# The second pass's mask of four heads copied into the bank by ScalarE, a third bank for its scores, and a third slice ahead of the projection

## The reference, cut to what matters

```python
scores = jnp.einsum('bhcqd,bhckd->bhcqk', qc, kb) / jnp.sqrt(jnp.asarray(d, q.dtype))
...
allowed = mb[:, None, :, None, :] & pos_ok[None, None, :, None, :] & band_ok[None, None, None, :, :]
scores = jnp.where(allowed, scores, jnp.asarray(-1000000000.0, scores.dtype))
probs = jax.nn.softmax(scores, axis=-1)
out = jnp.einsum('bhcqk,bhckd->bhcqd', probs, vb)
```

## Time and profile before

| | |
|---|---|
| median of 3 runs | 5509.81 us (5508.85 to 5511.06) |
| profiled execution, its own time | 5544.22 us |
| its span, first to last instruction | 5542.4 us |
| granted TensorE clock, mean | 0.978 of full speed |
| TensorE busy | 5064.9 us (91%) |
| VectorE busy | 3498.0 us (63%) |
| ScalarE busy | 2573.6 us (46%) |
| GpSimd busy | 1152.9 us (21%) |

### The profile page before, as it was taken

How to read it: one execution, slowest core, us unless ns; L and a number is a source line. 1 busy time by engine, 2 the same in 40 slices (tenths; PEclk the granted TensorE clock), 3 DMA queues, 4 the chain that set the end, 5 groups by cost and what they waited for, 6 DMA issues and landing times. The chain is left out here.

```text
span 5542.4 us, 119208 instructions
## 1 busy us (share of the span) xinstructions
PE 5064.9 (91%) x41842; PEld 3972.4 (72%) x41842; DVE 3498.0 (63%) x8963; ACT 2573.6 (46%) x5128; POOL 1152.9 (21%) x1048
## 2 busy tenths in 40 slices
PE   0799999999999999999999999969999954999999
PEld 0577777777777777777777777747777742777766
DVE  6566666666666666666666666567777745333332
ACT  0355555555555555555555555535555630111111
POOL 6111111111111111111111111100000001545453
PEclk9999999999999999999999999989999976999999
DMA  6544444444444444444544444344444420333232
GB/s 106 105 88 92 97 92 89 107 93 98 91 88 90 103 101 95 89 88 94 105 101 88 90 97 94 67 93 96 92 101 95 95 69 17 65 83 81 67 87 41
DMA packets 1283995, 488.94 MB, mean 88 GB/s; under 512 B 1086659, under 2 KB 1270560, under 8 KB 1283872
## 3 DMA queue, kind: packets, MB, share of 16 engines
q1 hardware_dynamic: 1256224, 450.63, 37.3%
q0 software_dynamic: 27648, 36.72, 4.3%
HBM read 162.82 MB, written 60.28 MB: 40 GB/s over the span
## 5 line engine op out<-in xcount | busy, mean ns | idle before, releaser
L764 ACT ACTIVATE pT<-banks 128x384 f32<-128x384 f32 x1920 | 924.9, 491 | 768.8 <-PE banks L533 758.1
L982 DVE TENSOR_REDUCE mx<-banks 128x4 f32<-128x768 f32 x768 | 719.4, 950 | 294.3 <-PE banks L514 294.3
L1165 POOL TENSOR_TENSOR rstd<-ve,half 128x2 f32<-128x2 f32 x288 | 218.8, 760 | 3062.4 <-DVE ve L891 3062.4
L496 PE MATMUL banks<-maskb,eyeb 128*128 128x384 bf16 (+1 forms) x2304 | 719.0, 312 | 91.6 <-DVE mx L986 27.0
L514 PE MATMUL banks<-qkT 128*128 128x192 bf16 (+2 forms) x3840 | 633.5, 247 | 0.0
L533 PE MATMUL banks<-qkT 128*128 128x192 bf16 (+2 forms) x3840 | 630.8, 247 | 0.0
L632 PE MATMUL banks<-w,pT 128*128 128x192 f32 x3072 | 554.5, 330 | 0.0
L632 PEld LDWEIGHTS banks<-w,pT 128*128 128x128 f32 x3072 | 492.7, 190 | 42.4 <-issue 21.9
L496 PE MATMUL banks<-mseq,eyeb 128*128 128x384 bf16 x1536 | 501.9, 327 | 9.1 <-issue 4.4
L618 PE MATMUL banks<-nT,w 128*128 128x256 f32 x1920 | 472.5, 382 | 6.6 <-DMA b<-in_b 3.1
L1910 PE MATMUL ps_g<-exp_xT,exp_wg 64*128 64x512 f32 x1152 | 466.8, 600 | 10.8 <-issue 5.4
(11 more groups left out here) (202 smaller groups left out, 8745.1 us busy)
## 6 DMA issues: line engine op xcount, KB each, us to landing
hcur<-hbuf SPq DMA_DIRECT2D x164, 192.0 KB
resid<-hbuf SPq DMA_DIRECT2D x160, 192.0 KB, 2.5
amb<-am_d SPq DMA_DIRECT2D x130, 192.0 KB, 3.0
hbuf<-hout SPq DMA_DIRECT2D x128, 192.0 KB, 2.0
exp_wg<-in_ewg SPq DMA_DIRECT2D x16, 768.0 KB
exp_wu<-in_ewu SPq DMA_DIRECT2D x16, 768.0 KB
exp_wd<-in_ewd SPq DMA_DIRECT2D x16, 576.0 KB
xs<-xr SPq DMA_DIRECT2D x32, 272.0 KB, 2.2
```

Of the source, the lines that this page charges most:

```text
L496: nc.tensor.matmul(part(dst), eyeb[:], part(mask), start=True, stop=ph is not tok)
L764: ph.inc(nc.scalar.activation(pT[s][:, h % NPT, :], bank[s][h % 2][:, 0:SCOLS], ACT.Exp, scale=SCALE), "p", s)
L982: last = nc.vector.tensor_reduce(mx[s][:, :, at].rearrange("p t h -> p h t"), src[:, :, 0:SCOLS].rearrange("p h (t k) -> p h t k", t=T), A ...
```

## The change

Four heads of K's second pass (7, 8, 9 and 11) get their mask from ScalarE, in the token layers only. After the Exp of head 6, ScalarE copies `mseq` into the banks of heads 7, 8 and 9, and after the Exp of head 10 into that of head 11; a new semaphore `wm` tells TensorE, which adds the two score matmuls to what stands there. The second pass of the token layers goes through banks 0, 1 and 3 in turn, so a head that TensorE masks waits for the Exp of head h-3. And of the six slices of the feed-forward three instead of two stand in front of the projection, here and in the causal block.

```diff
-UP_BEGIN = (0, 1)
-UP_REST = (2, 3, 4, 5)
+UP_BEGIN = (0, 1, 2)
+UP_REST = (3, 4, 5)
...
+WRITTEN = {6: (7, 8, 9), 10: (11,)}
+WRITTEN_HEADS = (7, 8, 9, 11)
...
+        def keys_bank(ph, s, h):
+            return bank[s][(0, 1, 3)[h % 3] if ph is tok else h % 2]
+
         def pe_scores2(ph, pe, K, V, h, kcols):
             s = K.s
+            written = ph is tok and h in WRITTEN_HEADS
+            ahead = 3 if ph is tok else 2
...
-            if h >= 2:
-                ph.wait(pe, "p", s, K.it, h - 1)
-            dst = bank[s][h % 2]
-            pe_mask(ph, dst, mseq[s] if ph is tok else maskb[:, 3, :])
+            dst = keys_bank(ph, s, h)
+            if written:
+                ph.wait(pe, "wm", s, K.it, WRITTEN_HEADS.index(h) + 1)
+            elif h >= ahead:
+                ph.wait(pe, "p", s, K.it, h + 1 - ahead)
+            if not written:
+                pe_mask(ph, dst, mseq[s] if ph is tok else maskb[:, 3, :])
...
-                ph.inc(nc.scalar.activation(pT[s][:, h % NPT, :], bank[s][h % 2][:, 0:SCOLS], ACT.Exp, scale=SCALE), "p", s)
+                ph.inc(nc.scalar.activation(pT[s][:, h % NPT, :], keys_bank(ph, s, h)[:, 0:SCOLS], ACT.Exp, scale=SCALE), "p", s)
+                for later in WRITTEN.get(h, ()) if ph is tok else ():
+                    ph.wait(act, "p", s, K.it, later - 2)
+                    ph.inc(nc.scalar.copy(keys_bank(ph, s, later)[:, 0:SCOLS], mseq[s][:]), "wm", s)
```

More of the change, by code:

```diff
@@ L441, in tower @@
         tok = Phase(layer_sems, dict(
-            common, tb=2, am_in=16, ms=1, ml=MASK_LINKS, hb2=1, w1_ps=FC, g=FC, w2_ps=1, r2=1, var2=1, rstd2=1, h2=1,
+            common, tb=2, am_in=16, ms=1, wm=len(WRITTEN_HEADS), ml=MASK_LINKS, hb2=1, w1_ps=FC, g=FC, w2_ps=1, r2=1, var2=1, rstd2=1, h2=1,
             h_st=16, sl=TOK_STACK_LINKS, fl=MAX_LINKS, bl=TOK_BACK_LINKS, b2=FFN_LINKS), "t",
@@ L534, in pe_scores2 @@
                                         qT[s][:, h, f0:f0 + w], start=False,
-                                        stop=(t == T - 1), skip_group_check=ph is not tok)
+                                        stop=(t == T - 1), skip_group_check=ph is not tok or written)
             ph.inc(last, "sc2", s)
```

## The result

The changed kernel takes 5434.83 us (5433.18 to 5438.39, 4 runs), the kernel before on the same chip 5510.44 (5508.85 to 5511.4): a ratio of 0.9864, 95% interval 0.9847 to 0.9881. That is 75.6 us less, where I forecast 69, and 5435 against 5441.

The account below looks back on a forecast made before the run. TensorE's issue was taken to bound the token stage; masks 0.36 plus slice 0.21 made 0.57 us a half, times 119 halves 68, plus 1 causal: 69 us off 5509.8, so 5441 us, likeliest range 5430 to 5456.

Parts of the forecast that it names:

- The factor of 119 halves: Of 128 token halves, 119 keep the gain; the last two and some 7 around layer changes do not.
- The masks: Token halves: four masks free 0.65 us of TensorE; waits of 0.07 (head 8) and 0.21 (head 10) leave 0.36.
- The copies: ScalarE's four mask copies per token half: 0.49 us each, spaced 0.39, costing nothing on the path.
- The price that the prediction put on slower copies: Slower rival, long copies into banks: gain gone at 0.7 us a copy, 1.2 us a half lost at 1.0; chance 0.04.
- The slice: Third slice before the projection removes TensorE's stall there for hT: 0.21 us a half, 0 if it only moves.
- The cover of the delayed norm: Behind the projection, residual and norm end 0.22 us later; 1.2 us remain before TensorE transposes h1.
- The sum: 0.36 + 0.21 = 0.57 us a half; over 119 halves 68 us, plus 1 in the causal stage: 69 us.
- ScalarE was not the limit: Rival: copy and Exp don't overlap, each taking 0.49 us; gain 0.34 a half, 40 us, 5469; chance 0.12.
- the slice gave its part: Rival: the third slice before the projection gives nothing; 0.36 a half, 43 us, 5467; chance 0.07.
- DMA didn't move in: Rival: DMA sets the pace, mT landing late and holding each half at some 0.2 of gain; 5486; chance 0.04.
- VectorE would be no limit: Rival: VectorE's maxima move too, so 0.86 us a half is gained, 102 us, 5408; chance 0.03.
- The granted clock: Waits of 0.07 and 0.21 shouldn't lower TensorE's clock; rival: half clock for parts of each half, 5630; chance 0.02.

Follow-up runs that it names:

- pool_late: The changed kernel, with POOL making the next masks only after all six row maxima of that half: 5404.50 us, 0.9805 of the kernel before.
- copy_twice: The changed kernel, with ScalarE copying each mask first into a spare tile nobody reads: 5554.35 us, 1.0081 of the kernel before.
- slice_only: The kernel before with only the third slice in front of the projection, masks and banks unchanged: 0.9942 of the kernel before (5509.99 us against 5543.66 us).
- three_masks: The changed kernel with head 11's mask given back to TensorE (ScalarE writes 7, 8, 9): 0.9868 of the kernel before (5470.92 us against 5543.66 us).
- five_masks: The changed kernel with head 6's mask also written by ScalarE, after the Exp of head 3: 5423.17 us, 0.9842 of the kernel before.

## Why the prediction was right, step by step

**What bounds.** TensorE's issue in the token stage, up to the dates that VectorE's maxima set: borne out by the runs; each change of a half's length in the traces is in the times. The factor of 119 halves was an estimate. By the traces the token stage gained some 123 times what a half gained here, and 122 times in `pool_late`.

**The masks**, 0.36 a half forecast. Head 10 came 0.362 and 0.363 earlier, with the two waits at their forecast places and sizes (0.07 and 0.21). Behind it half of the halves lose more: the transposes of hcur came 0.351 earlier in the first kind and 0.308 in the second, so 0.011 and 0.055 is lost there. I had them meet the fifth maximum to 0.01 us and took 0.01. `pool_late`, in which the fifth maximum comes earlier too, has both losses gone. In the mean the masks gave 0.330, 0.03 less than forecast.

**The copies**, 0.49 with a spacing of 0.39 forecast: 0.484 in the mean and 0.41 in the changed kernel, and no wait for them. `copy_twice` shows the cover and its end, and the walk made for it held within 3 us. The price that the prediction put on slower copies is too high: the gain gone at 0.7 us a copy and 1.2 lost at 1.0, so by the same slope of four 0.8 lost at 0.9, or 95 us. With 0.41 more for every copy, so about 0.9 each, a half was 0.435 and 0.362 longer than before, and the kernel 43 us slower. A straight line between the two kernels puts the break-even at about 0.73 (my estimate; no run measured it).

The Trainium skill ("ScalarE: Activation LUTs", What ACT_TABLE_LOAD costs) gives 186 ns plus 0.833 ns an element for an ACTIVATE with immediate operands, and an overlap of about 93 ns between two in a row. An estimate from these is 506 ns for 384 elements and a spacing of 0.41. The trace has 484 ns for the copy, which is what counts here, and the same spacing.

**The banks**: nothing forecast, 0.9993 of before measured.

**The slice**: 0.21 forecast. It is 0.206 in the first kind of half and 0.28 in the second (0.280 by the changed kernel's halves, 0.277 by `slice_only`), where the projection used to wait 0.08 longer. I had read one half of the first kind only. So this term was mis-sized too: 0.243 in the mean, 4 us in all. The cover of the delayed norm held: no wait of TensorE for h1 is in the waits.

**The sum.** 0.557 and 0.588 a half, 0.572 in the mean, against 0.57: the slice's surplus of 0.033 and the masks' shortfall of 0.030 cancel, so that the half came out this close is luck; the two mechanisms are not. The token stage gave 70.2 us by the two traces, where 68 was forecast, the causal stage 1.7 against 1, and the passage between them lost 1.4. That is 70.5 of the 75.6 us measured; the rest is inside the interval (66 to 84 us) and I can't assign it. The causal 1.7 isn't firm either: that stage takes 812.9 to 813.1 us in the three profiles with two slices ahead of the projection, and 810.2 to 813.2 in the eleven with three, 813.1 in `slice_only` among them.

**The profiled execution** was expected at 5473 and came out at 5431.4 because I took the profile's 34 us above the median for its own; they belong to the chip it was taken on.

**The rivals.** ScalarE was not the limit (0.41, not 0.49 a copy), the slice gave its part, DMA didn't move in. That VectorE would be no limit was out by `three_masks`. The granted clock stayed at 1.00 in both stretches above. Inside the four layers it was half for 3.4 us twice in the profile of the kernel before and twice in that of the changed one, each time just behind an idle of TensorE of 2.0 to 2.6 us around a change of layer, and not behind the waits of 0.07 and 0.21. The Trainium skill's rule on cycling through banks ("TensorE: Matmul & The Clock Gate", A second HAM failure mode: psum-queue depth-cycling) isn't seen at work in the halves of these two profiles.

**What I had not seen.** I wrote that behind the third maximum VectorE works without a break, and read its rows as its own time. This line of the profile before stands beside the centring (2015.02 to 2016.50) in the earlier trace rows:

```profile
2015.16 1.12 POOL L1175 TENSOR_TENSOR mseq<-maskf,amb 128x384 bf16<-128x384 f32 x1
```

Half of the centring's 1.48 us goes when POOL's mask is moved away. The forecast's dates came out, since the third maximum and the centring behind it don't move with the change. But the limit that took 0.21 us from each half was one of POOL against VectorE, and it could be had back for one wait: 31 us.

## What to carry to other kernels

A matmul taken out of a full TensorE is worth its slot only up to the next date that another engine sets; walk the half forward and look for these dates, because in front of such a wait a removed mask was worth 0 us, and 22 once the wait was gone. A spare half of an engine's span says nothing about a stretch: four copies were free and four more cost 118 us. Read both kinds of a repeating unit before sizing a stall.

## What the runs showed of the hardware

Two f32 instructions of 128 x 192 on VectorE (scalar_tensor_tensor, both tensors in SBUF) take 0.41 us each alone. In the changed kernel POOL's tensor_tensor of 128 x 384 runs beside both. The first meets it for its last 0.27 us and still takes 0.41; the second starts 0.18 behind POOL's start, takes 1.16 and ends 0.21 behind POOL's end, and POOL's takes 1.12 instead of 1.00. With POOL elsewhere the second is back to 0.41 in every half. The Trainium skill ("GPSIMD Engine Reference", the SBUF interfaces in its table of specifications) has VectorE instructions with two SBUF inputs contend with GpSimd. For the second instruction the trace agrees, and adds a size: 0.74 us lost by VectorE over an overlap of 0.94. Why the first loses nothing here (and 0.05 in `five_masks`), no run tells. The third maximum, which reads PSUM, takes 0.96 with POOL at work beside it and 0.96 without. The single durations are from the traces; the rows above merge the two instructions.

TensorE adds to a bank that ScalarE wrote, and starts 0.06 us after the copy's end when it has to wait for it.
